# One-hots all on VectorE, and the passes behind the edge sums at other steps

## The reference

```python
# block 0, graph part: 4 layers with 4 relations, each edge weighted by 1/(edges of its relation into its node)
h = einsum('ni,rio->rno', X, W);  msg = h[etype, src] * inv_deg[:, None]
out = segment_sum(msg, dst, N) + X @ root + bias
X = elu(layernorm(out) * gamma + beta) + X
# block 0, mixer part (on the same normalised rows xn)
q, k, v = xn @ Wqkv.T;  q = elu(q)+1;  k = elu(k)+1          # 8 heads of 32
t = (q @ (k.T v)) / (q @ sum(k) + 1e-6)
x1 = layernorm(t + xn);  x2 = layernorm(gelu(x1 @ W1.T + b1) @ W2.T + b2 + x1)
x = x + graph(xn) + x2;   x = x + routed_mlp(layernorm(x))
# block 1, graph part: 1 layer with 8 relations, unweighted, batch norm; then attention, gate and experts
agg = segment_sum(all_h[src, rel], dst, N)
```

## Time and profile before

| | |
|---|---|
| median of 3 executions | 8294.63 us |
| the profiled execution | 8290.02 us |
| its span, first to last instruction | 8288.2 us |
| around the span | 1.8 us |
| granted TensorE clock, mean | 0.824 of full |
| busy: PE, its weight loads, VectorE, ScalarE, POOL | 70%, 43%, 53%, 36%, 51% |
| sweeps A, B, C, D, E, first product to last add | 1168.3, 1151.9, 1350.1, 1044.3, 1037.8 us |

### The profile page before, as it was taken

One profiled execution on the slowest core, in us unless ns is written; L12 is line 12 of the kernel. 1 busy time (PEld: TensorE's weight loads), 2 busy tenths in 40 slices (PEclk: granted clock), 3 DMA queues, 4 the chain that ended last, 5 costly groups with the idle time before them and its releaser, 6 DMA issues. The chain is left out here.

```text
span 8288.2 us, 110504 instructions
## 1 busy us (share of the span) xinstructions
PE 5767.3 (70%) x17886; PEld 3544.0 (43%) x17886; DVE 4358.2 (53%) x14582; ACT 2952.1 (36%) x8048; POOL 4197.9 (51%) x4288
## 2 busy tenths in 40 slices
PE   0487777767777766666667777777498777764388
PEld 0244444444444444444443333355344444443265
DVE  7215555556666655555556666522433666652412
ACT  0134444434444445555543333322022444430132
POOL 0017666656666655555557777700001777762211
PEclk9798888888888888888886666588699888877699
DMA  1444444444444443333343333300044333330000
GB/s 55 144 134 122 123 121 120 122 121 134 134 134 133 131 120 115 112 115 111 116 128 109 104 104 104 99 11 0 13 137 133 105 105 105 105 92 2 12 15 18
DMA packets 478956, 811.01 MB, mean 98 GB/s; under 512 B 88600, under 2 KB 343148, under 8 KB 478657
## 3 DMA queue, kind: packets, MB, share of 16 engines
q0 software_dynamic: 200480, 548.02, 23.1%
q1 hardware_dynamic: 278430, 262.51, 9.7%
HBM read 614.04 MB, written 196.16 MB: 98 GB/s over the span
## 5 line engine op out<-in xcount | busy, mean ns | idle before, releaser
L522 POOL DMA_INDIRECT gnn_msg<-tables,gnn_row_ring x4165 | 3975.2, 954 | 2244.3 <-issue 1594.0
L571 PE MATMUL bank<-gnn_msg,gnn_hot 128*128 128x256 f32 x8330 | 3036.0, 489 | 1074.4 <-DVE sums L551 787.3
L551 DVE TENSOR_TENSOR sums<-sums,bank 128x256 f32 x4165 | 1749.3, 420 | 2037.4 <-PE bank L571 1502.4
L571 PEld LDWEIGHTS bank<-gnn_msg,gnn_hot 128*128 128x128 f32 x8330 | 1775.8, 237 | 2228.6 <-DVE sums L551 1519.1
L670 PE MATMUL bank<-gnn_w,residual 128*128 128x512 f32 x1176 | 657.8, 688 | 236.5 <-ACT residual L686 236.5
L133 POOL TENSOR_TENSOR ve<-mv,eps 128x7 f32<-128x7 f32 x35 | 7.1, 204 | 1341.0 <-DVE mv L127 1192.5
L512 ACT ACTIVATE gnn_hot<-gnn_away,gnn_meta_ring 128x128 f32<-128x128 f32 x1568 | 645.8, 482 | 47.3 <-ACT gnn_meta_ring L503 0.8
L500 ACT ACTIVATE gnn_away<-iota,gnn_meta_ring 128x128 f32<-128x128 f32 x1960 | 626.0, 390 | 58.1 <-ACT gnn_meta_ring L495 0.3
L531 DVE TENSOR_SCALAR gnn_hot<-iota,gnn_meta_ring 128x128 f32<-128x128 f32 x1764 | 620.6, 352 | 0.5 <-ACT gnn_meta_ring L495 0.5
L494 ACT COPY gnn_row_ring<-row 128x9 int32 (+1 forms) x490 | 97.8, 200 | 1425.7 <-PE bank L571 1413.7
L670 PEld LDWEIGHTS bank<-gnn_w,residual 128*128 128x128 f32 x1176 | 238.8, 214 | 482.2 <-ACT residual L686 299.2
(11 more groups left out here) (390 smaller groups left out, 6604.0 us busy)
## 6 DMA issues: line engine op xcount, KB each, us to landing
tables<-residual SPq DMA_DIRECT2D x294, 256.0 KB, 2.4
gnn_msg<-tables,gnn_row_ring POOLq DMA_INDIRECT x4165, 2.7
tables<-sums SPq DMA_DIRECT2D x98, 512.0 KB, 2.9
tables<-gnn_msg SPq DMA_DIRECT2D x98, 256.0 KB, 2.1
residual<-first_norm_columns SPq DMA_DIRECT2D x98, 128.0 KB
first_norm<-state SPq DMA_DIRECT2D x1, 6272.0 KB, 22.7
first_rows<-residual SPq DMA_DIRECT2D x1, 6272.0 KB, 39.3
residual<-first_norm SPq DMA_DIRECT2D x49, 128.0 KB
```

Of the source, the lines that this page charges most:

```text
L522: self.nc.gpsimd.indirect_dma_start(out=self.msg[:, s0 + u, :], out_offset=None, in_=table, in_offset=bass.IndirectOffsetOnAxis(ap=self.ro ...
L551: self.nc.vector.tensor_tensor(at, at, self.sums(s), ALU.add).then_inc(self.added, 1)
L571: self.nc.tensor.matmul(self.sums(s), self.hot[:, s, :], self.msg[:, s, :], start=True, stop=True).then_inc(self.summed, 1)
```

## The change

- **One-hots.** VectorE makes all 17 of a body; ScalarE's activations for them, their buffer `away` and their semaphores go, and `ring` is only its two copies. `NEXT_HOTS` has a one-hot behind each of steps 1 to 8 for the own second half, and nine behind steps 11 to 16 for the next body's first half, two of them behind 11, 14 and 16. Each still comes ahead of the hooks of its step.
- **Root in pieces.** The 12 instructions come four each behind steps 1, 2 and 3. In E (`Keys1`) they stay together.
- **A step for each pass.** `Post.vector`: L625 moves to step 4, L628 to 5, L631 from 6 to 7, L639 from 7 to 8, L642 from 15 to 14. `Post.tensor`: transposes from 9 to 11; then the root product alone behind 12 (into bank 1, no longer after an eviction), and the four halves of the two relation products behind 13, 14, 15 and 16, the first two into bank 3, the last two into bank 1 once the base (L642) has read it.
- **`Keys0`, `Attend`, `Feed`.** TensorE's first product of `Keys0` and of `Attend` from 3 to 5, `Feed`'s transposes from 1 to 3 and its first product from 3 to 6. TensorE's second product from 11 (`Keys0`), 8 (`Attend`) and 6 (`Feed`) to 10. VectorE's pass that it needs from 8 to 9 (`Keys0`, L800) and from 5 to 9 (`Attend`, L950); `Feed`'s comes from ScalarE. The norm's passes on VectorE are spread over steps 3, 6, 9 and 10, those that end the tile over 12, 13 and 15.
- **ScalarE's queue.** The ring of the second half now stands between the two evictions L690.

```diff
-NEXT_HOTS = (((), (), (0,), (), (1,), (), (2,), (), (3,)),
-             ((), (), (0,), (1,), (), (2,), (3,), (4,)))
+NEXT_HOTS = (((), (0,), (1,), (2,), (3,), (4,), (5,), (6,), (7,)),
+             ((), (), (0, 1), (2,), (3,), (4, 5), (6,), (7, 8)))
 # ring(): the copies stay, all behind them goes
-        act.wait_ge(self.ring_ready, n * 4 + (2 * h + 2))
-        for k in range(ACT_HOTS): ... activation(self.away[:, k, :], self.c.iota[:], ACT.Abs, ...)
-        self.nc.scalar.mul(m[:, :, 2], m[:, :, 1], -1.0)
-        for k in range(ACT_HOTS): ... activation(to, self.away[:, k, :], ACT.Relu, ...)
 # Post.vector
-            if s == 1:
-                dve.wait_ge(self.s_mv, n)
-                inverse_root(dve, c, ..., self.s_root, n - 1)
-            if s == 2:
+            if s in (1, 2, 3):
+                if s == 1:
+                    dve.wait_ge(self.s_mv, n)
+                root_steps(dve, c, ..., self.s_root, n - 1, 4 * (s - 1), 4 * s)
+            if s == 4:
                 v.scalar_tensor_tensor(self.u, agg, ...).then_inc(self.s_u1, 1)
+            if s == 5:
                 dve.wait_ge(self.s_u1, n)
...
-            if s == 6:
+            if s == 7:
                 dve.wait_ge(self.s_exp, n)
...
-            if s == 7:
+            if s == 8:
                 dve.wait_ge(self.s_elu, n)
...
-            if s == 15 and not last:
-                dve.wait_ge(self.s_prod, n * 3)
+            if s == 14 and not last:
+                dve.wait_ge(self.s_prod, n * 3 - 2)
 # Post.tensor
-            if s == 9:
+            if s == 11:
                 pe.wait_ge(self.s_new, n)
...
-            if s in (11, 12):  # both halves of relation product j = s - 11, bank 1 + 2 * j
-            if s == 14:        # root product, after s_out >= n * 2 + 1
+            if s == 12:
+                pe.wait_ge(self.s_xt, n)
+                pe.wait_ge(self.s_base, n)
                 for h in range(KH):
                     ins = t.matmul(c.bank[1][:, 0:D], self.xt[:, h, :], self.w[:, h, REL0 * D:], ...)
                 ins.then_inc(self.s_prod, 1)
+            if s in (13, 14, 15, 16):
+                j, h = (s - 13) // KH, (s - 13) % KH
+                if s == 15:
+                    pe.wait_ge(self.s_base, n + 1)
+                ins = t.matmul(c.bank[3 - 2 * j][:], self.xt[:, h, :], self.w[:, h, j * 512:(j + 1) * 512], ...)
+                if h == KH - 1:
+                    ins.then_inc(self.s_prod, 1)
 # Keys0.tensor                                  # Keys0.vector
-            if s == 3 and first:
+            if s == 5 and first:
-            if s == 11 and first:                -            if s == 8 and first:
+            if s == 10 and first:                +            if s == 9 and first:
                 pe.wait_ge(self.s_k, i + 1)
                 pe.wait_ge(self.s_real, i + 1)
 # Attend.tensor                                 # Attend.vector
-            if s == 8 and first:                 -            if s == 5 and first:
+            if s == 10 and first:                +            if s == 9 and first:
                 pe.wait_ge(self.s_q, i + 1)
 # Feed.tensor
-            if s == 3 and first:
+            if s == 6 and first:
                 pe.wait_ge(self.s_xt, i + 1)
-            if s == 6 and first:
+            if s == 10 and first:
                 pe.wait_ge(self.s_act, i * 2 + 3)
 # Feed.vector, end of the tile: L1077 9 to 12, L1079 9 to 13, end_first 9 to 15
 # gnn0, ScalarE
                         edges.ring(act, i + 1, n + 1, 0)
-                        post.scalar(act, n, t)
+                        post.turned(act, n, t)
+                        post.way_out(act, n, 0)
                         edges.ring(act, i + 1, n + 1, 1)
+                        post.way_out(act, n, 1)
```

`root_steps` issues instructions `begin` to `end` of the same 12, each after a wait for the one before it, and after the last one waits for its end:

```diff
+def root_steps(dve, c, y, half, t, var, s_step, i, begin, end):
+    v = c.nc.vector
+    first = i * ROOT_STEPS
+    for k in range(begin, end):
+        if k:
+            dve.wait_ge(s_step, first + k)
...
+        ins.then_inc(s_step, 1)
+    if end == ROOT_STEPS:
+        dve.wait_ge(s_step, first + ROOT_STEPS)
+        gate(dve, c)
```

More of the change, by code:

```diff
@@ L538, in begin_vector @@
         dve.wait_ge(self.ring_ready, n * 4 + 2)
-        for u in range(DVE_HOTS[0]):
+        for u in range(HALF):
             self.one_hot(0, u)
@@ L686, in scalar, with way_out @@
         sc.copy(self.xt.rearrange("p h r -> p (h r)"), c.bank[3][:, 0:D]).then_inc(self.s_xt, 1)
-        for j in range(2):
-            act.wait_ge(self.s_store[j], n * 16)
-            act.wait_ge(self.s_prod, n * 3 + (j - 2))
-            sc.copy(self.outs[:, j, :], c.bank[1 + 2 * j][:]).then_inc(self.s_out, 1)
+    def way_out(self, act, n, j):
+        act.wait_ge(self.s_store[j], n * 16)
+        act.wait_ge(self.s_prod, n * 3 + (j - 1))
+        self.nc.scalar.copy(self.outs[:, j, :], self.c.bank[3 - 2 * j][:]).then_inc(self.s_out, 1)
     def sync(self, sp, n, t, table):
@@ L775, in after @@
                 ins.then_inc(self.s_mm, 1)
-            if s == 11 and first:
+            if s == 10 and first:
                 pe.wait_ge(self.s_k, i + 1)
@@ L797, in after @@
         def after(s):
-            if s == 8 and first:
+            if s == 9 and first:
                 dve.wait_ge(self.s_act, i * 3 + 4)
@@ L956, in after @@
                 v.tensor_tensor(self.done, self.u, self.vec[:, 1, :], ALU.add).then_inc(self.s_done, 1)
-            if s == 11 and first:
+            if s == 12 and first:
                 both = c.bank[2][:, 0:KH * (P + 4)].rearrange("p (s m) -> p s m", s=KH)
@@ L968, in after @@
                                 self.z.unsqueeze(3).to_broadcast([P, KH, 4, 32]), ALU.mult).then_inc(self.s_t, 1)
+            if s == 13 and first:
                 dve.wait_ge(self.s_t, i + 1)
@@ L971, in after @@
                 v.tensor_tensor(self.u, self.u, self.x, ALU.add).then_inc(self.s_u, 1)
+            if s == 15 and first:
                 self.end_first(dve, i)
@@ L1027, in after @@
         def after(s):
-            if s == 1 and first:
+            if s == 3 and first:
                 pe.wait_ge(self.s_dma, i * 16 + 16)
@@ L1072, in after @@
                 v.tensor_tensor(self.done, self.u, self.first_x, ALU.add).then_inc(self.s_done, 1)
-            if s == 9 and first:
+            if s == 12 and first:
                 if second:
@@ L1092, in gnn0 @@
         vecs = sb("vecs", [P, 3, D], F32)
[L1093 removed]
         row_ring = sb("row_ring", [P, 2, HALF], I32)
[L1095 removed]
+        meta_ring = sb("meta_ring", [P, 2, HALF, 2], F32)
         own = sb("own", [P, 2 * D + 16], F32)
@@ L1104, in gnn0 @@
         edges = c.edges = EdgeSum(nc, c)
-        edges.use(msg, hot, away, row_ring, meta_ring, c.row4, True)
+        edges.use(msg, hot, row_ring, meta_ring, c.row4, True)
         post = Post(nc, c, ph, cutter(own), scratch, vecs, w)
@@ L1300, in _ @@
                     work.scalar(act, NT, False, True)
-                    post.scalar(act, (l + 1) * NT, t)
+                    post.turned(act, (l + 1) * NT, t)
+                    for j in range(2):
+                        post.way_out(act, (l + 1) * NT, j)
                 for h in range(2):
```

112 lines of the change are left out of this document (37 added, 75 removed).

## The result

The changed kernel takes **8413.95 us** (median of 4, 8406.87 to 8415.79) against 8294.28 us beside it: ratio **1.0142**, 95% interval 1.0126 to 1.0158. Forecast were 8340 us and a loss of 47; the loss is 119.7. The profiled execution has a span of 8405.1 us against 8288.2.

A forecast was written before the change was run, and what follows sets the result against it. A to C were taken as bound by a closed chain over VectorE, TensorE and ScalarE, D and E by POOL. A +1.45, B +2.0, C -2.75 times 49 made +34; with +10 and +3, +47: 8340 us (8225 to 8450).

The forecast's parts named there:

- VectorE's prices: Start-to-start costs on VectorE: add to add 0.63 us, add to one-hot 0.34, one-hot to next pass 0.26.
- TensorE's wait at step 10: In A and B TensorE idles about 4 us for VectorE's pass behind the register load, with the transposes queued behind.
- I let its first 3.3 us of work run at half clock: In A and B, TensorE's work after the wait at step 10 runs at half clock for 3.3 us.
- 0.6 a body for short register loads: One VectorE register load in four is 1.2 us shorter, taking 0.6 us off the average body.
- link 3: In A to C, ScalarE's copy of the transposed tile; forecast 0.4 us after the transposes instead of 2.8.
- C: Sweep C: 24.8 us a body against 27.55, a change of -2.75.
- D and E: Sweeps at the pace of POOL's gathers, about 21.25 us a body; the change does nothing for both.
- Rival (c): POOL pays: each added one-hot holds up a gather by 0.34 us, also in D and E; about 8600 us; 3%.
- Sweep ends +3: The root product ahead of the tables delays three sweep ends by 0.9 us: +3 us.
- Rival (a): In A and B TensorE restarts at full clock, 1.4 us a body, 137 in all; 8205 us; 18%.
- Rival (b): In A and B half clock lasts to the ring's end, 1.2 us more on 98 bodies; 8460 us; 12%.
- main case: A and B lengthen through TensorE's wait, C shortens; 8340 us, own range 8290 to 8395; 62%.

The follow-up runs named there:

- pass8: Changed kernel with VectorE's pass of sweeps A and B behind step 8 again instead of step 9, ahead of the register load; 8193.2 us.
- sp_early: Changed kernel with SP's load issues moved between the two table stores of the body before, the second store waiting until TensorE passed step 4; 8397.7 us.
- kept_warm: Changed kernel with four extra 512-column products, sums unused, on TensorE ahead of its wait at step 10 in A and B; 8238.0 us.
- steps_only: Changed kernel's steps with the one-hots shared as before the change, nine on VectorE and eight on ScalarE; 8557.0 us.
- load_late_b: Changed kernel with a second set of nine registers for the first half's tile numbers, loaded behind step 10 of the body before; 8252.5 us.
- best1: Changed kernel with Keys0 at its old steps, Attend's pass behind step 8, and in B the first half's register load behind the previous body's step 10; 8132.7 us.
- ka_old: Changed kernel with Keys0 and Attend at their old steps, the norm's shift staying behind step 3; 10257.4 us on a slow chip, 8287.4 repeated elsewhere.
- best3: best1 with two extra 512-column products, sums unused, on TensorE ahead of step 10's wait in B; 10141.3 us on a slow chip, 8134.2 repeated elsewhere.

## Why the prediction was wrong

The direction, the place and the mechanism held; the size of the loss did not (47 forecast, 120 measured). Two terms of the sum for A and B were too small: the half clock behind the wait at step 10 (1.4 us counted, 2.1 measured) and the start of the body (3.1 to the first add, 3.74 measured, since SP's DMA issues were put at nothing). By its steps:

- **VectorE's prices**: held. From add 0 to L616 the forecast has 10.0 and the trace 9.99; add 8 to add 9 forecast 2.77, measured 2.65; add 14 with two one-hots to the base 0.85 against 0.85.
- **First add 3.1 after the first product**: failed, it is 3.74 (B 3.78, C 3.57). The new place of the second eviction brings SP's issues into the register load. The prediction counted no issue of SP's there. Taken out, the load is shorter by 0.64, and the kernel by 16 us.
- **TensorE's wait at step 10**: held, 4.01 for "about 4". pass8 shows that it is the loss in A and two thirds of that in B.
- **"I let its first 3.3 us of work run at half clock"**: this is the term that failed most. The clock rows have 4.5 us at half behind the restart in A and 4.3 in B, the mean of 46 bodies, and 6.0 in the body of sp_early shown. In the 23 bodies of A with both loads long the mean is 27.22 in the changed kernel and 25.11 in kept_warm: the half clock costs 2.1 where 1.4 was counted. The forecast had 25.9 for such a body; 0.64 from the start and 0.7 from the clock give 27.2.
- **0.6 a body for short register loads**: the mean of the bodies of A is 0.9 below the long ones, and the sweep divided by 49 lies another 0.2 below that mean, since its first body, without `Post`, takes 20.9. The two take back part of that miss. So A is off by 0.83 a body, B by the same: 81 us, less 10 for C. The 10 us for one-hots lengthened by a gather don't show as a part of their own, and 15 us in place of 3 lie outside the sweeps.
- **ScalarE's one-hots gone, worth it in link 3**: the copy is early as forecast, 0.67 after the transposes (forecast 0.4; they ran at half clock) where it was 2.8. What that alone is worth was not measured: the one-hots are worth 47 us with the old steps, and 143 with the new ones, where steps_only lost by SP's late column load.
- **C**: held, 24.60 against 24.8; L841 starts at 10.3 where L863 was forecast at 9.7. **D and E**: held. D has 388 more VectorE instructions and is no longer. Rival (c) fails by that: gathers keep 1.25 us in D (1040.6 / 49 / 17).
- **Sweep ends +3**: 14.7 lie outside the sweeps, 11.7 of them in code between D and E and behind E that the change doesn't touch; not traced further.
- **Rival (a)** was priced at 137 for full clock; kept_warm measures 176 for it, by making it happen. **Rival (b)**, 8460, was nearer than the main case: the truth lies between them.

For rival (c) the prediction named a page. The Trainium skill (SBUF — State Buffer, section "Who interferes with whom") lets whoever comes second block. The trace shows one side of it: a one-hot that begins 0.4 us after a gather's start takes some 0.53 us instead of 0.34 in D, and the gathers' starts stay 1.25 us apart in the median with none, one or two one-hots beside them.

Why the slow stretch differs behind the same wait of 4 us is seen in the clock rows. The clock falls during the wait, but not at the same place in it, and comes back that much earlier or later behind the restart: 4.5 and 6.0 us in the two bodies above, 2.8 to 6.2 over A of the changed kernel where it was at half at the restart. So 0.4 to 0.5 us won ahead of the wait can be taken back whole, as in B of sp_early, while the 2.3 to 2.8 of load_late_b could not. A length for one body can't be forecast from the wait alone; what stays open is why B's mean rose from 4.3 to 4.8 and A's from 4.5 to 4.7 only.

## What to carry to other kernels

When a pass is moved one step, look at what the sequencer does between the steps: a register load that no busy time counts stood between step 8 and step 9, and put a wait of 4 us on another engine. Price a wait of TensorE with the half clock behind it as a range, not as one length, and look in the clock rows where in the wait the clock fell; filling the wait with work that is thrown away shows its price in one run. And judge a spread of steps sweep by sweep: here each of three bodies wanted another order, and the best kernel takes one from each. When a kernel takes a fifth longer on another chip, read the sequencers' rows there before naming a cause: the transfers looked like it and were not.

## What the runs showed of the hardware

- VectorE's load of nine registers takes 2.07 us, and 2.71 with two DMA issues of SP beside it. That is 230 and 300 ns a register. About one load in four is short, 0.84 us for nine.
- On the same point the Trainium skill (Runtime: NRT & Kernel Launch, section "Instruction fetch mechanics") has about 200 ns a register for register loads. The trace is near it for the long loads, above it beside SP and below it for the short ones.
- The granted clock falls while TensorE stands for 4 us and is at half for 4.3 to 4.8 us behind it in the mean of a sweep (A and B of the changed kernel and sp_early). Four products thrown away in that wait are worth 1.7 us a body; two in a wait of 2.07 (B of best1) are worth nothing to the body.
- On two of the chips the same kernel takes 9899 and 10091 us instead of 8294. In the traces of ka_old and best3, taken there, some 1100 of VectorE's sequencer instructions take about 0.70 us each; those of L148 take 0.04 elsewhere. POOL's gathers and their packets have their usual length.
